# Mixture of experts on one core: the gather of the next tile's rows placed behind the down products in TensorE's queue

## The reference, cut to what matters

```python
# x: 512 tokens of 512; 16 experts; W1 (16, 512, 1024), W2 (16, 1024, 512)
probs = softmax(xt @ Wr + br);  w, idx = top_k(probs, 2);  w = w / sum(w)
comb[token, idx] += w
h = gelu(einsum('td,edh->teh', xt, W1) + b1)
o = einsum('teh,eho->teo', h, W2) + b2
y = xt + einsum('teo,te->to', o, comb)
```

## Time and profile before

| | us |
|---|---|
| median of 3 runs | 2964.33 (2954.12 to 2964.47) |
| the profiled execution | 2963.49 |
| its span, first to last instruction | 2961.7 |
| TensorE busy in the span | 2448.7 (83%) |
| VectorE busy | 1913.8 (65%) |
| ScalarE busy | 1589.4 (54%) |
| GpSimd busy | 943.5 (32%) |

### The profile page before, as it was taken

One profiled execution on the slowest core, in us unless ns is written; L12 is line 12 of the kernel. 1 busy time (PEld: TensorE's weight loads), 2 busy tenths in 40 slices (PEclk: granted clock), 3 DMA queues, 4 the chain that ended last, 5 costly groups with the idle time before them and its releaser, 6 DMA issues. The chain is left out here.

```text
span 2961.7 us, 56486 instructions
## 1 busy us (share of the span) xinstructions
PE 2448.7 (83%) x21354; PEld 1586.9 (54%) x21666; DVE 1913.8 (65%) x4197; ACT 1589.4 (54%) x2918; POOL 943.5 (32%) x724
## 2 busy tenths in 40 slices
PE   4489999999999999995787799873899999958624
PEld 2235555555555556554344677651667677744312
DVE  4578777777777766661112799964777776631285
ACT  3336656666665665554122688753477777761021
POOL 2303233333323342223000233324467666550000
PEclk8699999999999999998997799986999999968857
DMA  3311121112111110001200799845434332213020
GB/s 116 96 31 40 33 79 47 37 33 78 45 32 34 62 37 5 5 3 68 82 29 4 255 343 345 307 145 164 150 112 128 112 122 86 86 34 110 30 88 14
DMA packets 197327, 268.64 MB, mean 91 GB/s; under 512 B 48945, under 2 KB 124849, under 8 KB 196545
## 3 DMA queue, kind: packets, MB, share of 16 engines
q1 hardware_dynamic: 193104, 256.88, 26.0%
q10 hardware_dynamic: 3312, 6.03, 0.5%
q0 software_dynamic: 640, 2.10, 0.3%
HBM read 221.18 MB, written 43.78 MB: 89 GB/s over the span
## 5 line engine op out<-in xcount | busy, mean ns | idle before, releaser
L544 POOL TENSOR_TENSOR a_plo<-a_p,a_phi 128x512 bf16<-128x512 f32 x272 | 315.5, 1160 | 817.8 <-ACT a_phi L600 817.2
L736 PE MATMUL ps<-w_hi,a_xlo 128*128 128x512 bf16 x1085 | 414.2, 382 | 1.9
L735 PE MATMUL ps<-w_lo,a_xhi 128*128 128x512 bf16 x1052 | 402.5, 383 | 3.0 <-issue 0.2
L734 PE MATMUL ps<-w_hi,a_xhi 128*128 128x512 bf16 x1034 | 395.3, 382 | 0.6 <-DVE a_v L623 0.4
L1846 POOL TENSOR_TENSOR a_plo<-a_p,a_phi 128x512 bf16<-128x512 f32 x256 | 303.1, 1184 | 192.0 <-ACT a_phi L1883 186.7
L566 ACT ACTIVATE a_kraw<-ps 128x256 f32<-128x256 f32 x272 | 104.2, 383 | 413.0 <-PE ps L736 408.1
L623 DVE TENSOR_TENSOR a_v<-ps,a_v 128x256 bf16<-128x256 f32 x272 | 114.7, 422 | 261.8 <-ACT a_v L568 260.3
L1958 DVE CUSTOM_DVE_ANT_0 a_junk<-ps,a_biasrow 128x512 bf16<-128x512 f32 x256 | 176.1, 688 | 116.0 <-PE ps L2063 86.6
L1878 ACT ACTIVATE a_p<-ps,a_mcol 128x512 f32<-128x512 f32 x256 | 175.0, 684 | 101.6 <-PE ps L2081 95.1
L596 ACT ACTIVATE a_p<-ps,a_mcol 128x512 f32<-128x512 f32 x256 | 175.3, 685 | 57.4 <-PE ps L787 57.2
L668 DVE CUSTOM_DVE_ANT_0 a_junk<-ps,a_mrow 128x512 bf16<-128x512 f32 x256 | 174.4, 681 | 13.4 <-PE ps L765 12.6
(11 more groups left out here) (436 smaller groups left out, 7114.7 us busy)
## 6 DMA issues: line engine op xcount, KB each, us to landing
e_wst<-in_L_ffn_W SPq DMA_DIRECT2D x46, 2048.0 KB, 9.6
a_xn<-in_ctx SPq DMA_DIRECT2D x16, 1024.0 KB, 5.6
a_ct<-in_ctxT SPq DMA_DIRECT2D x16, 1024.0 KB, 6.1
a_ks<-k1h_d SPq DMA_DIRECT2D x128, 128.0 KB, 2.4
k1h_d<-a_khi SPq DMA_DIRECT2D x64, 128.0 KB, 2.0
k1l_d<-a_klo SPq DMA_DIRECT2D x64, 128.0 KB, 1.7
a_ks<-k1l_d SPq DMA_DIRECT2D x64, 128.0 KB, 2.6
xh_d<-a_xshi SPq DMA_DIRECT2D x48, 128.0 KB, 1.8
```

Source lines behind the costliest of these rows:

```text
L544: pool.tensor_tensor(p_lo[:, m % 3, :], p32[:, m % 2, :], p_hi[:, m % 3, :], ALU.subtract)\
L734: pe.matmul(out, x_hi[:, c, tile], w_hi[:, c, g, :], start=(c == 0), stop=False)
L735: pe.matmul(out, x_hi[:, c, tile], w_lo[:, c, g, :], start=False, stop=False)
L736: last = pe.matmul(out, x_lo[:, c, tile], w_hi[:, c, g, :], start=False, stop=(c == C - 1))
```

## The change

In TensorE's loop `down(q - 1)` is issued ahead of `gather(q + 1)` instead of behind it. For q = 0 there is no down, and for q = 22 no gather, so 21 turns are changed. No other queue is touched.

```diff
@@ -1561,10 +1561,10 @@
                 if q == 1:
                     pe.wait_ge(y_done, B)
                 up(q)
+                if q:
+                    down(q - 1)
                 if q + 1 < TILES:
                     gather(q + 1)
-                if q:
-                    down(q - 1)
             down(TILES - 1)
```

## The result

| | us |
|---|---|
| before, median of 4 runs | 2964.40 (2954.12 to 2965.78) |
| changed, median of 4 runs | 2998.42 (2996.66 to 2999.54) |
| ratio changed to before | 1.0122, 95% interval 1.0098 to 1.0145 |
| span of the profiled execution, before and changed | 2961.7 and 2994.9 |

A forecast was written before the change was run, and what follows sets the result against it. VectorE, with its stall behind GpSimd's product, was taken to bound the kernel; 2963.5 + 26.6 for the new loop's turns + 6 for the clock = 2996.1 us, own range 2984 to 3008, over all cases 2978 to 3016.

The forecast's parts named there:

- The bound before: VectorE was taken as nearly full in the expert stage: 9.6 us of own work a tile, the rest GpSimd's product.
- port stall: VectorE and GpSimd exclude each other at SBUF; the later stands still, 3.3 to 3.9 us a tile for VectorE.
- The loop: Gather half, ScalarE's `gathered` and `down_high`, GpSimd's `down_low` half, TensorE's `down`, next gather: 14.99 us a plain turn against 13.11.
- TensorE's own chain: TensorE's up, down and gather with handovers and `gathered_low`: 13.5 us a turn in both kinds of tile.
- Overflow tiles: Turns in which `choose` lasts 1.86 us instead of 0.60, so GpSimd ends later: 15.92 us against 15.61.
- The clock: TensorE's pauses may lower its clock: nothing charged for plain tiles, half of seven overflow tiles, +6 us.
- The ends: Second `gathered_low` +1.7 us later behind a down block; after tile 22, GpSimd's last product -1.7 us; they cancel.
- The sum: 13 turns of 14.99 and 7 of 15.92 us make 306.3, minus 279.67 is +26.6; the clock adds 6.
- TensorE's chain alone: Rival: GpSimd's product is through early, so only TensorE's chain sets the turn, 13.5 us; 2954 us in all; chance 5%.
- GpSimd did stand behind `down_low`: The rival denied that GpSimd's product waits for VectorE's `down_low`: 12.7 us drop out, about 2977 to 2983; chance 7%.

## Why the prediction was right

- *The bound before.* VectorE with the port stall: shown by the cut of GpSimd's work (12.32 us turns, TensorE full) and by the output copy's move (16 us off). TensorE's own parts add up to 12.49 us, not the 12.4 of the prediction; in the queue they take 12.32.
- *The loop.* 14.99 us worked out, 15.03 measured. Its parts: VectorE's `gathered_low` to `down_low` 1.53 us on both sides; GpSimd's end to the second down matmul 0.28 worked out and 0.31 measured; the product with its wait 4.39 (0.31 + 4.08); `down` 5.18. That it is a loop through ScalarE and GpSimd is shown from two sides: cut at ScalarE or at the gather's high half it gives 13.47, with GpSimd's work taken away 13.47. TensorE's own chain was put at 13.5.
- *Overflow tiles.* 15.92 worked out, 15.96 measured where the clock held.
- *The clock.* Nothing for plain tiles: right, 0.99 to 1.00. Half of seven dips at 1.7 us, 6 us, was a little low: five at 1.6 to 1.7, 8 us. "Half" was a choice between the bounds and not worked out, so that it came within 2 us is partly luck.
- *The ends.* The first changed turn was to bring +1.7 us: the distance from the first `gathered_low` to the second grew from 12.91 to 14.72, +1.8. GpSimd's last product was to end 16.4 us after the last `gathered_low`; it ends at 2019.75 + 4.36 = 2024.11, 16.35 after 2007.76.
- *The sum.* 306.3 + 6 = 312.3 us for the 20 turns, 315.3 measured (279.67 before), so +35.6 in the stage against +34.0 in the medians. In the profiled execution of the changed kernel the stage also began 2.1 us later, ahead of any changed instruction, and the stages behind it took 4.7 us less; these two are not explained. So the stage cost 3 us more than was worked out, and what happened outside it gave 2.6 back: that the total of the profiled execution, 2996.66, is so near to 2996.1 is luck to that extent.
- *The rivals.* TensorE's chain alone is what was left once the loop was cut; even then plain tiles are not faster than before (13.47 against 13.11). GpSimd did stand behind `down_low` (5.31 us rows). The Trainium skill's rule (SBUF — State Buffer, "Who interferes with whom") says also that the order of issue decides who blocks: the rows show both orders, GpSimd held for 0.3 to 1.9 us and VectorE for 2.5 to 3.9.

The expectations that failed are, above all, those of the overflow tiles of the three kernels with the loop cut at ScalarE or at the gather. I had computed a mean load of VectorE; a stall of up to 3.9 us in front of `gathered_low` is not a mean but a matter of a few tenths of a microsecond in which GpSimd or VectorE comes first, and it brings a clock dip with it. Two kernels came out below their ranges: the kernel before with little work for GpSimd, whose turns are 12.32 us and not 12.5 to 13.0, and the one with the output copy on ScalarE, whose plain turns are longer than expected but whose overflow turns are 1.6 us shorter than in the kernel before (13.99 against 15.61 in the mean).

## What to carry to other kernels

Moving work behind a block in an in-order queue is to be priced by who reads its result and what stands behind those readers in their own queues: here a copy of 0.6 us carried 3.7 us of other work and a second engine's 4.1 us behind it, back to the very block that was moved ahead. Close the loop on paper, add its parts, and compare with the pitch of a tile; busy shares do not show it, since every engine had free time in the slower kernel. And where two engines share a port, put an instruction that does not use it, or a wait that is there anyway, where the other one gets in: here the output copy took 0.6 us of the stall, and VectorE's wait for the gather hid 2.5 us of it. Which product stands still matters as well: the same stall cost a turn most on `gelu_low`, in front of the copy for which TensorE waits.

## What was unexpected of the hardware

- The same three waits of TensorE in another order made a handover 0.16 us longer (0.47 instead of 0.31 us from GpSimd's end to the second matmul), and the turn with it, 15.03 to 15.19. With matmuls between the waits, or with one of them missing, it was 0.31 and 0.32.
- A tiny product is held up at the port like a large one: the first instruction of an overflow tile's `choose`, 128 x 8 numbers with one input from SBUF, takes 0.15 us by itself. In the kernel before, GpSimd's product having started 0.04 us ahead of it, it took 4.08 us:

```profile
1859.51 4.09 POOL L1264 TENSOR_TENSOR e_wlo<-e_wst,e_whi 128x2048 bf16<-128x2048 f32 x1 [9.44 <-ACT e_whi L1287]
```

```profile
1859.55 4.08 DVE L1368 TENSOR_SCALAR e_ds<-e_d 128x8 f32<-128x8 f32 x1
```

- The loads moved 363 GB/s over 163 us, with the DMA engines 0.99 busy, without holding up TensorE at its floor; in the kernel before they moved 338.
- A stall at the port can set the clock: a `gelu_low` that came 0.33 us too late cost 3.9 us at the port, and TensorE's pause of 3.74 us was followed by a lower clock (0.95 over the overflow tiles of that kernel).
